# A recommendation model's gathers: the clamped row in 128 copies, and gathers that wait only for their own buffers

## The reference

```
h = relu(dense @ dw1 + db1); dense_emb = relu(h @ dw2 + db2)            # 2048 x 64
sparse_emb = emb_tables[f_ids, sparse_idx]                              # 26 tables of 12500 rows x 64
emb = concatenate([dense_emb[:, None, :], sparse_emb], axis=1)          # 2048 x 27 x 64
inter = einsum('bfd,bgd->bfg', emb, emb)                                # all dot products of a sample
pairs = inter[:, iu0, iu1]                                              # the 351 above the diagonal
z = concatenate([emb.reshape(B, -1), pairs], axis=1)
z = relu(z @ ow1 + ob1); z = relu(z @ ow2 + ob2); z = relu(z @ ow3 + ob3)
return z @ ow4 + ob4                                                    # widths 512, 256, 128, 1
```

## Time and profile before

| | |
|---|---|
| median of 3 runs | 709.89 us (705.44 to 711.31) |
| span of the profiled execution | 704.8 us |
| gathers, POOL | 416 instructions, 392.6 us |
| PE matmul | 484.0 us busy |
| DVE, ACT | 151.4 and 148.4 us busy |
| DMA queue of the gathers | 13.66 MB, 23.2% of 16 engines' span |
| mean granted clock of TensorE | 0.818 |

### The profile page before, as it was taken

How to read it: one execution, slowest core, us unless ns; L and a number is a source line. 1 busy time by engine, 2 the same in 40 slices (tenths; PEclk the granted TensorE clock), 3 DMA queues, 4 the chain that set the end, 5 groups by cost and what they waited for, 6 DMA issues and landing times.

```text
span 704.8 us, 5797 instructions
## 1 busy us (share of the span) xinstructions
PE 484.0 (69%) x2262; PEld 265.8 (38%) x2262; DVE 151.4 (21%) x295; ACT 148.4 (21%) x334; POOL 392.8 (56%) x420
## 2 busy tenths in 40 slices
PE   4864928659286693938759487693937938597788
PEld 1223414334143342424334243342414423254666
DVE  1021302122030221402222030320402213131223
ACT  2312203121111312203122121212203122121312
POOL 6756464764647466564764647466464665647330
PEclk9986967959589596977959789596976979779799
DMA  8522231221313222131221213223231231322110
GB/s 250 98 20 23 19 23 15 26 22 17 22 15 26 20 19 23 18 23 16 24 23 17 22 16 26 20 19 22 18 24 16 21 22 18 22 18 26 12 14 2
DMA packets 17167, 19.39 MB, mean 28 GB/s; under 512 B 7359, under 2 KB 8386, under 8 KB 17127
## 3 DMA queue, kind: packets, MB, share of 16 engines
q0 software_dynamic: 13312, 13.66, 23.2%
q1 hardware_dynamic: 3408, 5.02, 2.1%
q10 hardware_dynamic: 420, 0.34, 0.2%
HBM read 18.99 MB, written 0.01 MB: 27 GB/s over the span
## 4 chain that ended last, share of the span: by engine, by line
another core or an unknown queue 42%; PE 34%; DVE 11%; issue 9%; ACT 4%; DMA 0%; DVEq 0%
PE l_ps L678 9%; PE gram_ps L657 8%; PE l_ps L686 8%; DVE slots L291 4%; DVE gram_c L315 2%; PE l_ps L669 2%; PE tr_ps L640 1%; DVE feat L282 1%; DVE pairs L296 1%; PE l_ps L772 1%; PE tr_ps L621 1%; DVE h1t L303 1%; ACT slots L443 1%; ACT gram_c L455 1%
## 5 line engine op out<-in xcount | busy, mean ns | idle before, releaser
L247 POOL DMA_INDIRECT emb<-table_dram,rows x416 | 392.6, 944 | 287.1 <-issue 117.0
L678 PE MATMUL l_ps<-w_sb,feat 128*128 128x512 f32 x390 | 197.9, 656 | 13.9 <-DVE feat L282 7.2
L657 PE MATMUL gram_ps<-slots 64*128 64x108 f32 x960 | 88.8, 352 | 144.1 <-DVE gram_c L315 139.5
L657 PEld LDWEIGHTS gram_ps<-slots 64*128 64x128 f32 x960 | 81.6, 258 | 161.7 <-DVE gram_c L315 145.0
L678 PEld LDWEIGHTS l_ps<-w_sb,feat 128*128 128x128 f32 x390 | 77.6, 209 | 120.8 <-issue 110.5
L315 DVE COPY gram_c<-gram_ps 32x432 f32<-32x432 f32 x60 | 36.5, 609 | 343.4 <-remote 275.5
L455 ACT COPY gram_c<-gram_ps 32x432 f32<-32x432 f32 x60 | 30.5, 508 | 305.5 <-remote 262.8
L686 PE MATMUL l_ps<-w1p_sb,pairs 118*128 118x512 f32 x90 | 53.4, 740 | 14.4 <-DVE pairs L296 11.9
L621 PE MATMUL tr_ps<-ident_sb,emb 128*128 128x128 f32 x203 | 36.6, 291 | 23.9 <-DMA emb<-table_dram,rows 13.5
L443 ACT COPY slots<-tr_ps 64x256 f32<-64x256 f32 (+1 forms) x128 | 50.3, 393 | 1.1
L621 PEld LDWEIGHTS tr_ps<-ident_sb,emb 128*128 128x128 f32 x203 | 26.6, 149 | 53.8 <-issue 35.9
(11 more groups left out here) (103 smaller groups left out, 202.9 us busy)
## 6 DMA issues: line engine op xcount, KB each, us to landing
emb<-table_dram,rows POOLq DMA_INDIRECT x416
w_sb<-ow_dram SPq DMA_DIRECT2D x3, 1024.0 KB, 7.4
w1p_sb<-ow_pairs_dram SPq DMA_DIRECT2D x1, 708.0 KB
w_sb<-ow_dram SPq DMA_DIRECT2D x1, 512.0 KB
w_sb<-ow_dram SPq DMA_DIRECT2D x1, 256.0 KB
idx_raw<-idx_dram ACTq DMA_DIRECT2D x1, 208.0 KB, 2.7
w1d_sb<-ow_dram SPq DMA_DIRECT2D x1, 128.0 KB
w_sb<-ow_dram SPq DMA_DIRECT2D x1, 128.0 KB
```

The lines of the kernel that those rows point to most:

```text
L247: pool.indirect_dma_start(out=emb[:, t % RING, c // 2, c % 2 * D:(c % 2 + 1) * D], out_offset=None, in_=table, in_offset=bass.IndirectOffs ...
L657: mm = nc.tensor.matmul(gram_ps[:, bank, r * GCOLS:(r + 1) * GCOLS], x.rearrange("p c f -> p (c f)"), x[:, :, 0:SLOTS], start=True, stop=True)
L678: nc.tensor.matmul(l1_ps[t % 2][:], feat[t % 2][:, n - 1, :], w1_sb[:, n - 1, :], start=False, stop=False)
```

## The change

Each table gets 127 further copies of its last row behind its end, so a table has V + 127 rows and the last row lies there 128 times. The upper clamp is no longer the constant V - 1 but one value per partition, V - 1 + p, read from a new tile `last_row_sb` that one more DMA on SP fills. The bases grow accordingly. DVE waits for this load too before it clamps. And POOL's waits are replaced: group n of tile t waits, from tile 4 on, for the transposes of the same group four tiles earlier, whose buffer it overwrites. Nothing of the PE, ACT or layer code is touched.

```diff
@@ -75,6 +76,7 @@
         first_sb = sb("first_sb", [P, 2, NF], I32)
+        last_row_sb = sb("last_row_sb", [P, 1])
@@ -219,6 +222,7 @@
             sp.dma_start(first_sb[:], first).then_inc(first_in, 16)
+            sp.dma_start(last_row_sb[:], last_row).then_inc(last_row_in, 16)
             sp.dma_start(ident_sb[:], ident).then_inc(ident_in, 16)
@@ -241,8 +245,8 @@
                 pool.wait_ge(rows_in, min(t, 1) + 1)
                 for n, (a, b) in enumerate(GROUPS):
-                    if t >= 1:
-                        pool.wait_ge(transposed, t * NG + (-2, 0, 1, 2)[n])
+                    if t >= RING:
+                        pool.wait_ge(transposed, (t - RING) * NG + n + 1)
@@ -255,6 +259,7 @@
                     dve.wait_ge(first_in, 16)
+                    dve.wait_ge(last_row_in, 16)
@@ -266,7 +271,7 @@
-                nc.vector.scalar_tensor_tensor(out=rows[:, a:b, :], in0=f, scalar=float(V - 1), in1=base,
+                nc.vector.scalar_tensor_tensor(out=rows[:, a:b, :], in0=f, scalar=last_row_sb[:], in1=base,
                                                op0=ALU.min, op1=ALU.add).then_inc(rows_in, 1)
@@ -888,19 +893,21 @@
+    table = _np.concatenate([x["emb_tables"], _np.repeat(x["emb_tables"][:, -1:], P - 1, axis=1)], axis=1)
-    base = _np.tile(_np.arange(NF, dtype=_np.int32) * V, (P, 1))
+    base = _np.tile(_np.arange(NF, dtype=_np.int32) * (V + P - 1), (P, 1))
-        "table_dram": x["emb_tables"].reshape(NF * V, D),
+        "last_row_dram": _np.arange(V - 1, V - 1 + P, dtype=_np.float32)[:, None],
+        "table_dram": table.reshape(-1, D),
```

More of the change, by code:

```diff
@@ L26, in bass_dlrm_kernel @@
     first: bass.AP,
+    last_row: bass.AP,
     table: bass.AP,
@@ L111, in bass_dlrm_kernel @@
         first_in = sem("first_in")
+        last_row_in = sem("last_row_in")
         idx_in = sem("idx_in")
```

## The result

The changed kernel took 771.4 us (median of 4 runs, 767.8 to 774.2) against 710.5 us for the kernel before (705.4 to 711.3) on the same chip: ratio 1.088, 95% interval 1.084 to 1.092, slower. The forecast was 548 us with a range to 695; the result is rival B's 775 within 0.5%. The profiled execution spans 772.4 us against 704.8.

A forecast was written before the change was run, and what follows sets the result against it. A 42.5 us tile was 29.0 us of PE's chain plus 13.5 us of hold; without it POOL's issue bounds: tile 14's last gather landed at 492.6, + 56.6 = 549.2, less clock gains 547, taken as 548 us; range 535 to 695.

The forecast's parts named there:

- rival B: The hold stays because long gather runs cause it, not their rows; 775 us, chance 0.20.
- the hold goes with the hot ones: Step blaming gathers of mostly one row for late PE completions; spreading rows would remove 13.5 us from 13 tiles.
- the hold: PE's finished products and transposes told late, together, just after a gather run's last rows land; 13.5 us a tile.
- hot gathers: Gathers of 21 features, about seven in eight rows clamped to the table's last; DMA share about 0.37.
- cold gathers: Gathers from tables 0, 2, 3, 18 and 24, their 128 rows all different; DMA share 0.12.
- Rows spread: Part giving the last row 128 copies; hot gathers should look cold, DMA share 0.12 to 0.15 instead of 0.37.
- landing gain: Spread rows land sooner after issue: 1.2 us a group, at most 18 us in all, bounds 0 to 18.
- Waits: POOL waiting only for the buffer four tiles back runs free; worth what is left above 32.5 us a tile.
- Start: One more SP load before the first gather moves it by 0.46 us to 4.6; bounds 0.4 to 2 us.
- POOL's pace: POOL issues 416 gathers in one unbroken run at 1.249 us each, which sets the pace.
- the floor: Last gather's rows landed at 525.0 plus 15.9 us after the last group's transpose: 540.9 us.
- PE's chain: PE's own work per tile without the hold, a stretch at 1.2 GHz included: 29.0 us.

The follow-up runs named there:

- e1: Kernel before with only the 128 copies of the last row, POOL's old waits kept; 710.7 us against 705.4, ratio 1.008.
- e2: Kernel before with only the new POOL waits, last row in one place; 769.5 us, ratio 1.092.
- e10: Changed kernel, each gather fetching rows for partitions 0 to 63 alone, the rest zero; 800.5 us against 713.3, ratio 1.123.
- e7: Changed kernel plus a 160-column POOL memset behind each gather; 589.9 us against 543.2 for the kernel before, ratio 1.086.
- e14: Changed kernel plus a 384-column POOL memset behind each gather; 667.8 us against 707.9 for the kernel before, ratio 0.943.
- e4: Changed kernel plus a 256-column POOL memset behind each gather; 633.8 us against 705.4 for the kernel before, ratio 0.900.
- e12: Kernel before with the new waits and a 256-column POOL memset behind each gather, last row in one place; 710.6 us, ratio 0.996.
- e17: Changed kernel plus three 2048-column POOL memsets behind each tile's 26 gathers; 762.0 us, ratio 1.071 to the kernel before.
- e18: Changed kernel run again unedited; 789.7 us against 712.4 for the kernel before, ratio 1.111.
- e13: Changed kernel plus a 256-column POOL memset behind each gather, e4 again; 641.2 us against 707.9, ratio 0.905.
- e16: Same kernel as e12 in another group of runs; 649.7 us against 707.9 for the kernel before, ratio 0.917.

## Why the prediction was wrong

*The step that failed* is "the hold goes with the hot ones". The DMA share of hot windows and the place of the hold in the run agreed, and I took the one for the cause. But hot gathers stand late in every tile, so place in the run explained it as well; rival B said so, and I gave it 0.20. e1, e2 and e10 show that the rows have no part in the 1.40 us. My arguments against B fall too. The lower DMA share came and the hold stayed. Completions that pass with cold gathers in flight did so just after a pause, when the queue was short. That they also pass at once 20 us into tile 0's run a plain queue doesn't explain, though: 16 x 0.15 = 2.4 us should be seen there.

Nor is it first in, first out. Timelines after the change, DVE and then PE:

```profile
47.77 0.69 DVE L287 COPY feat<-tr_ps 128x512 f32<-128x512 f32 x1 [40.80 <-remote]
...
84.80 0.29 DVE L287 COPY feat<-tr_ps 128x128 f32<-128x128 f32 x1 [34.69 <-issue]
```

```profile
32.37 0.60 PE L626 MATMUL tr_ps<-ident_sb,emb 128*128 128x128 f32 x4
...
53.58 0.71 PE L626 MATMUL tr_ps<-ident_sb,emb 128*128 128x128 f32 x5
...
113.48 0.33 PE L662 MATMUL gram_ps<-slots 64*128 64x108 f32 x1 [2.47 <-issue]
```

In the middle of the long run transposes that ended at 33.0 are answered at 47.8, and those of 54.3 at 81.3 (ACT) and 84.8. The Gram products that ended at 113.8 are told only at 187.0. By then 88 gathers had been issued; in a queue served in order their completion would come at about 5.0 + 88 x 1.40 = 128 us, an estimate from the table's numbers. So the 1.40 us tell when the queue is empty, and that a completion mostly waits until then; how it takes its turns before stays open.

*What the trace of before could have told.* The 1.40 us stood in it as PE's spacing inside a hold, and I used it only as a sign of the hold. Set beside POOL's 1.249 it predicts a backlog, which a run of another length would have borne out. The kernel before has one, tile 0's 26 gathers (timeline of before):

```profile
35.46 0.94 POOL L247 DMA_INDIRECT emb<-table_dram,rows  x1 [0.31 <-issue]
40.29 0.69 DVE L282 COPY feat<-tr_ps 128x512 f32<-128x512 f32 x1 [34.25 <-remote]
```

Release 4.8 us after the last issue, against 4.1 after 18 gathers: and (40.2 - 4.1) / 26 = 1.39 us per gather.

*Rows spread*: share 0.10 to 0.15, as said. The landing gain of up to 18 us was 0 (e1), within its bounds.

*Waits*: the direction was wrong. They were priced at what is left over POOL's 32.5 us; they kept the runs short. B's price was right in sum and not in its parts: the first run was 130 gathers, not 112, since the transposes of tile 0 that the ring waits for had been told by 84.8, before POOL asked for them (+ 22.5 us), and the release came 20.9 us after the last issue, not 2.5 (+ 18.4). From the end of the first hold, as B counts, the loss was 187.0 - 40.2 = 147 us in place of 107, and 147 - 68 = 79 came back in place of 37; the two errors cancelled.

*Start*: first gather at 5.00, forecast 4.6. DVE started at 4.03 on the new load, 0.80 after the 3.23 of before, not 0.46; inside the bounds.

*POOL's pace* 1.249 and the floor: right (1.249; and e7 and e14 end 18.3 and 18.2 us behind the start of their last gather, for which the forecast summed 2.1 + 15.9 = 18.0). *PE's chain*: tiles 12 to 14 took (731.28 - 643.36) / 3 = 29.3 us without a hold, forecast 29.0; but singly they are 26.3, 30.7 and 31.0, and the first starts from a copy that was still held, so the agreement of the mean is partly luck.

*The trace records.* The Trainium skill, "NOTIFIC — the notification-queue block", section 7.1, says that the block pushes back on its producers inside its own pipeline rather than lose a record. Completions that are held whatever the rows (e1, e2, e10) would fit a path that fills by the number of items. No run here shows which path it is. Every run on record comes with the granted clock of its core, and none is known to have been made without recording, so whether the kernel is held when nothing is recorded is a question that no run here answers.

## What to carry over

When several waits end together and no instruction explains them, look for a queue: divide the time from a run's first item to the release by the items in it, and see whether the quotient is the same for runs of other lengths. If the issuer is faster than that quotient, a wait that looks needless may be what drains the queue, and taking it away lengthens the run and the hold. Slowing the issuer just past the quotient paid here where both parts of the change did not (633.8 us against 705.4, e4), but not everywhere: e12 gained nothing by it (710.6 against 713.3), and in the group of runs without the queue it cost 15% (624 against 543).

## What the runs showed of the hardware that was not expected

- Gathers of one column each are served at 1.40 us apiece (1.400 to 1.403 over 130), for 128 or 64 rows, one row or many, while POOL issues them at 1.21 to 1.25. While the queue is not empty, completions of PE and of POOL's own memsets can be late, and PE steps at 1.40 us per instruction. Not all are: 20 us into the first run they still pass at once.
- The kernel before took 543.1 to 543.4 us in one group of runs and 699 to 720 in the others (medians 705 to 713). In the one group none of the four kernels run showed a hold. The group's chip had the same number as that of e17 and e18, where before took 712; so the number doesn't decide it, and what does is open.
- With 21 of 26 features mostly on one row queue 0 was busy 23.2% of the span, with the row in 128 copies 7.5%. The copies brought nothing at the kernel's own pace (e1, 0.8% slower), and about 8 us where the gathers were paced (e13 and e16).
